# What GpSimd waits for while it scatters the input rows of a routed FFN

## The chip, the cores and the metric

One Trainium2 chip, one core. The metric is the device time of one execution in microseconds. The runs of the kernel before have a median of 1396.52 us (three runs, 1396.34 to 1397.36).

## The reference

Four sequences of 512 tokens with 256 values each (2048 rows, float32) pass through four residual layers, each behind a layernorm:

```python
x = x + attn_a(layernorm(x))        # 32 query heads, 8 key heads, rotary, causal
x = x + ffn(layernorm(x))           # routed
x = x + attn_b(layernorm(x))        # 16 differential heads, causal
x = x + ffn(layernorm(x))           # the same weights again
```

The FFN has 16 experts of inner width 176. Each token chooses four of them (out of its two best groups of four). With weights from a softmax over all experts,

```python
y = sum over the 4 chosen e of weight[e] * W2[e] @ (silu(W1[e] @ x) * (W3[e] @ x))
z = Ws2 @ (silu(Ws1 @ x) * (Ws3 @ x))      # the shared expert, inner width 352, every token
out = y + z
```

## The kernel before

The kernel is written engine by engine. Each engine has one list of instructions in program order, and the lists meet in semaphores: an instruction adds to one when it is done, and another engine's `wait_ge` holds that engine until the value is reached. Here are the parts of an FFN layer. The first FFN is called "f" in the code, the second "h".

**Seam.** TensorE projects the attention's output tile by tile, VectorE adds it to x, ScalarE normalises, and TensorE computes the router's logits. A row of `y_sb` then holds the normalised input (256 values), four slot numbers, four weights and the token's own row number: 265 values, 1060 bytes.

**Routing.** VectorE chooses the experts (`choose`), and `assign` (L1313) turns the choices into slot numbers in `slot_i`. Slots are places in the DRAM array `x_slots`, in which the rows of one expert lie together. `e_slots` goes up once for each half of the 16 tiles of 128 tokens.

**Dispatch.** GpSimd (`pool_ffn`) issues 64 indirect DMAs at L675, one for each tile of 128 tokens and each of the four choices. Each writes 128 rows of 1060 bytes from `y_sb` to the places given in `slot_i`. Scatter n belongs to tile n // 4. The first 40 (EARLY_T = 10 tiles) add to semaphore `scat0` when they land, the last 24 to `scat1`, 16 for each DMA. Between them stand waits: the table SHARED_AT names eleven scatters (8, 12, ..., 48), and before each of them GpSimd waits at L674 until the shared expert has come a given number of steps (`f_hw_used` or `h_hw_used`).

**Shared expert.** It runs at the same time in 12 steps, three for each sequence. In a step TensorE computes both inner products (L1909, eight matmuls), ScalarE applies the SiLU (L879), VectorE multiplies (L1414), and TensorE multiplies with Ws2 (L1919, eight matmuls, then `hw_used` goes up). After every third step VectorE adds the result to x (L1402). VectorE's remaining routing work (`full_tiles`, `places`, `order`) is spread between these steps.

**Experts.** The slots form 72 tiles of 128 rows, dealt with in 36 pairs. SyncE (`sp_ffn_slots`) waits for the landing of all 40 early scatters, then for each tile j reads the tile's first row from SBUF into a register (L490) and loads the tile into one of eight buffers `xg` (L465). With every second tile it also reads the expert's number (L511) and loads a part of that expert's W2 (L512). Before tile 4 it stores the last quarter of x (L486). Tiles from 24 on (EARLY) may also hold late tokens, so before tile 24 SyncE waits for `scat1`. Ahead of the steady work for the first pair, SyncE thus goes through: load 0, load 1, late weights, load 2, load 3, late weights, store of x, load 4, load 5. TensorE transposes each tile (L1941), multiplies with W1 and W3 (L1966), transposes the product (L1973), and multiplies with W2 (L1999 to L2004). Its loop for pair p begins with the transposes of pair p+2. ScalarE empties the transposes (L883) and applies the SiLU (L888), VectorE multiplies (L1439, L1442), finds each row's weight and destination (L1468 to L1482), and scales the result into one of eight buffers `yt` (L1456). Eight of the 72 tiles hold two experts' rows and have a second scatter.

**Results.** GpSimd adds each result tile to the output rows in DRAM, with 80 indirect accumulating DMAs at L691 (`scatter_out`). They stand behind the dispatch's 64 scatters in GpSimd's list. VectorE may fill a `yt` buffer again only when the scatter of its tile eight places before has landed. At the end SyncE loads the sums back (L524).

The change touches `pool_ffn` alone, and in it `scatter`:

```python
if n in SHARED_AT:
    pool.wait_ge(sm(f + "_hw_used"), 2 + SHARED_AT[n])
```

Of the kernel before, what the change touches and what calls it, by code (L numbers as in the profile page):

```python
# [26 lines left out]
NT = B * TB  # L27
# [26 lines left out]
TOPK = 4  # L54
# [19 lines left out]
EARLY_T = 10  # L74
# [5 lines left out]
assert EARLY * P <= EARLY_T * P * TOPK - NE * (P - 1)  # L80
SCH = [(0, 128), (128, 128), (256, 96)]
M_DMAS = 2 * 16
SHARED_AT = {8: 2, 12: 3, 16: 4, 20: 5, 24: 6, 28: 7, 32: 8, 36: 9, 40: 10, 44: 11, 48: 12}


class Chain:
# [13 lines left out]
def build(nc, ins, out):  # L100
    ctx = ExitStack()
    with ctx:
# [3 lines left out]
        def sem(name):  # L106
            return ctx.enter_context(nc.semaphore(name))
# [157 lines left out]
        def sm(name):  # L265
            if name not in S:
                S[name] = sem(name)
            return S[name]
# [65 lines left out]
        def past(f, n):  # L334

            return n if f == "h" else 0
# [331 lines left out]

        def pool_ffn(pool, f):

            def scatter(n):
                t, k = n // TOPK, n % TOPK
                if n in SHARED_AT:
                    pool.wait_ge(sm(f + "_hw_used"), 2 + SHARED_AT[n])  # L674
                pool.indirect_dma_start(x_slots, bass.IndirectOffsetOnAxis(ap=slot_i[:, t, k:k + 1], axis=0),  # L675
                                        y_sb[:, t, :], None).then_inc(sm("scat0" if t < EARLY_T else "scat1"), 16)

            outs = [(j, h) for j in range(NJ) for h in range(1 + (j in MIX))]

            def scatter_out(s):  # L680


                if s >= ACCS:
                    i, h = outs[s - ACCS]
                    if h == 0:
                        pool.wait_ge(sm(f"store{i % XR}"), 16 * (i // XR + 1 + past(f, NJ // XR)))
                    else:
                        pool.wait_ge(sm("store_second"), 16 * (MIX.index(i) + 1 + past(f, MIXED)))
                j, h = outs[s]
                to = j if h == 0 else NJ + MIX.index(j)  # L690
                pool.indirect_dma_start(y_acc[f][s % ACCS], bass.IndirectOffsetOnAxis(ap=dest[:, to:to + 1], axis=0),  # L691
                                        yt[:, j % XR, :], None, compute_op=ALU.add)\
                    .then_inc(sm(f"store{j % XR}" if h == 0 else "store_second"), 16)

            def result_out(j):
                pool.wait_ge(sm("e_dest"), j // 4 + 1 + past(f, NJ // 4))
                pool.wait_ge(sm("e_y_ev"), j + 1 + past(f, NJ))
                if j == 0:
                    pool.wait_ge(sm("acc_x"), 16 * B * (1 + past(f, 1)))
                scatter_out(outs.index((j, 0)))  # L700
                if j in MIX:
                    scatter_out(outs.index((j, 1)))

            pool.wait_ge(sm("e_slots"), 1 + past(f, 2))
            pool.wait_ge(sm("cleared"), 16 * (SLOT_ROWS // (4 * P) + 22))
            for n in range(TH * TOPK):
                scatter(n)
            pool.wait_ge(sm("e_slots"), 2 + past(f, 2))
            for n in range(TH * TOPK, NT * TOPK):
                scatter(n)  # L710
            for j in range(NJ):
                result_out(j)

        @block.gpsimd
        def _(pool):
            pool.memset(zero, 0.0).then_inc(sm("zeroed"), 1)

            pool.memset(v_all[:, :, :, D:D + 1], 1.0).then_inc(sm("a_ones"), 1)
            pool.wait_ge(sm("a_ones"), 1)
            pool_attn(pool, "a")  # L720
            pool_ffn(pool, "f")
            pool_back(pool)
            vo = v_all.rearrange("p g t (h c) -> p g t h c", h=2)
            pool.memset(vo[:, :, :, :, 16:17], 1.0).then_inc(sm("b_ones"), 1)
            pool.wait_ge(sm("b_ones"), 1)
            pool_attn(pool, "b")
            pool_ffn(pool, "h")
# [1388 lines left out]
```

## Time and profile before

| | us |
|---|---|
| median of three runs | 1396.52 |
| the profiled execution | 1398.89 |
| its span in the profile | 1397.2 |
| busy in the span: TensorE | 1153.5 (83%) |
| VectorE | 873.7 (63%) |
| GpSimd | 689.9 (49%) |
| ScalarE | 542.6 (39%) |
| DMA bytes, mean rate | 177.42 MB, 127 GB/s |

The profile shows one execution. PE is TensorE, DVE VectorE, ACT ScalarE, POOL GpSimd, SP SyncE; a "q" behind a name is the engine's instruction queue (waits, register work, DMA issues). Times are microseconds from the start of the span. In a timeline a row has start, duration (of the whole group, where several instructions are merged), engine, line, operation, output<-input, count, and in square brackets how long the engine was idle before and what ended that. "issue" means that the profile shows nothing it waited for, "remote" that the release came from no instruction the profile could name. The busy time of a GpSimd scatter is the time to make its descriptors, not that of the transfer. The two FFN layers begin their dispatch at 404.5 and 1087.0 us.

### The profile page before, as it was taken

The page shows a single profiled execution, that of the slowest core. Times are in us where ns is not written, and L with a number is a line of the kernel's source. Part 1 is how long each engine was busy: PE and PEld are TensorE (multiplying, and loading weights), DVE is VectorE, ACT ScalarE, POOL GpSimd, SP SyncE. Part 2 cuts the span into 40 slices and gives each one's busy share as a digit, 9 for nine tenths or more (in the row PEclk, how much of TensorE's full clock was granted, in tenths as well). Part 3 has the DMA queues.
Part 4 walks back from the last instruction along what each step waited for, and adds up shares of the span by engine and source line. Part 5 has one row for each costly group of instructions (what it writes and reads, how often), then busy time and mean ns, then how long its engine had stood idle before and what let it go on. Part 6 is the DMA issues. An engine that isn't in the chain of part 4 may idle for free.

```text
span 1397.2 us, 25837 instructions
## 1 busy us (share of the span) xinstructions
PE 1153.5 (83%) x8690; PEld 619.0 (44%) x8690; DVE 873.7 (63%) x2061; ACT 542.6 (39%) x846; POOL 689.9 (49%) x841
## 2 busy tenths in 40 slices
PE   6888899997888469999568799999878974999990
PEld 2343343332754246665233344444246542666550
DVE  5588888881783035555288799999567611555453
ACT  2125777778511012222122377777844100222210
POOL 4452344454036736677553355454520674667771
PEclk9887999999889679999779999999998995999995
DMA  4424655510813358888664422221062334788868
GB/s 148 130 83 146 191 185 180 160 44 26 287 42 121 133 125 151 151 153 145 110 194 152 149 54 54 61 58 51 3 233 47 109 128 129 140 152 154 156 91 255
DMA packets 154353, 177.42 MB, mean 127 GB/s; under 512 B 20016, under 2 KB 139760, under 8 KB 153712
## 3 DMA queue, kind: packets, MB, share of 16 engines
q1 hardware_dynamic: 124336, 136.38, 33.2%
q0 software_dynamic: 29184, 38.36, 16.2%
q8 instruction: 73, 1.20, 0.3%
q10 hardware_dynamic: 704, 1.02, 0.2%
q14 instruction: 56, 0.46, 0.1%
HBM read 91.12 MB, written 83.78 MB: 125 GB/s over the span
## 4 chain that ended last, share of the span: by engine, by line
PE 54%; DVE 17%; issue 8%; SPq 5%; ACT 5%; DMA 4%; POOL 4%; another core or an unknown queue 1%; POOLq 0%; ACTq 0%; DVEq 0%
PE pair_ps L1966 11%; PE o_ps L1737 8%; DVE nm L1106 4%; PE pair_ps L1999 4%; ACT arena L832 3%; DVE bm L1106 3%; POOL x_slots L675 3%; PE pair_ps L2002 2%; PE t_ps L1763 2%; PE pair_ps L1687 2%; PE pair_ps L1568 2%; PE pair_ps L1973 2%; DMA arena<-mT 2%; PE pair_ps L1662 2%; PE pair_ps L1667 2%
## 5 line engine op out<-in xcount | busy, mean ns | idle before, releaser
L832 ACT ACTIVATE arena<-pair_ps 128x1024 f32<-128x1024 f32 x320 | 323.5, 1025 | 134.0 <-PE pair_ps L1662 79.4
L615 POOL TENSOR_SCALAR_AFFINE_SELECT arena<-arena 128x512 f32<-128x512 f32 (+1 forms) x320 | 175.8, 549 | 243.2 <-ACT arena L832 242.7
L1106 DVE TENSOR_REDUCE nm<-pair_ps 128x2 f32<-128x1024 f32 (+1 forms) x192 | 232.9, 1222 | 37.2 <-PE pair_ps L1711 33.6
L675 POOL DMA_INDIRECT x_slots<-y_sb,slot_i x128 | 123.5, 965 | 168.7 <-DVE slot_i L1313 117.7
L1737 PE MATMUL o_ps<-arena 128*9 128x512 f32 (+7 forms) x2048 | 177.0, 441 | 4.3 <-POOL arena L615 4.1
L1966 PE MATMUL pair_ps<-arena 128*128 x512 | 170.1, 474 | 6.1 <-issue 6.1
L691 POOL DMA_INDIRECT y_f<-xnT,dest x80 | 125.0, 1563 | 72.4 <-DVE xnT L1456 51.7
L691 POOL DMA_INDIRECT y_h<-xnT,dest x80 | 124.7, 1559 | 67.9 <-DVE xnT L1456 43.5
L1106 DVE TENSOR_REDUCE bm<-pair_ps 128x8 f32<-128x1024 f32 x128 | 155.4, 1218 | 4.5 <-PE pair_ps L1711 1.0
L1439 DVE TENSOR_TENSOR arena<-arena,pair_ps 128x128 f32<-128x128 f32 x144 | 41.5, 288 | 128.5 <-ACT arena L888 77.3
L1966 PEld LDWEIGHTS pair_ps<-arena 128*128 128x128 f32 x512 | 95.2, 197 | 48.6 <-issue 11.8
L888 ACT ACTIVATE arena<-pair_ps 128x176 f32<-128x176 f32 x144 | 45.7, 318 | 168.4 <-PE pair_ps L1966 84.2
L1909 PE MATMUL pair_ps<-arena 128*128 128x512 f32 (+1 forms) x192 | 92.2, 627 | 0.0
L1456 DVE TENSOR_SCALAR xnT<-pair_ps,slot_w 128x256 f32<-128x256 f32 x144 | 64.5, 480 | 42.0 <-PE pair_ps L2004 24.0
L1711 PE MATMUL pair_ps<-c_b 64*128 64x128 bf16 (+1 forms) x1280 | 85.1, 210 | 0.0
L1711 PEld LDWEIGHTS pair_ps<-c_b 64*128 64x128 bf16 x1280 | 60.8, 98 | 33.8 <-issue 4.7
L1687 PE MATMUL pair_ps<-arena 48*128 48x512 bf16 x256 | 51.6, 397 | 20.8 <-ACT arena L832 16.5
L1662 PE MATMUL pair_ps<-arena 51*128 51x512 bf16 x256 | 51.2, 396 | 21.3 <-DMA arena<-mT 8.6
L879 ACT ACTIVATE sil<-pair_ps 128x512 f32<-128x512 f32 (+1 forms) x24 | 14.2, 596 | 124.7 <-PE pair_ps L1909 80.9
L1737 PEld LDWEIGHTS o_ps<-arena 128*9 128x9 f32 (+1 forms) x2048 | 39.0, 93 | 53.3 <-issue 30.3
L1999 PE MATMUL pair_ps<-arena 128*128 x224 | 59.1, 386 | 0.0
L883 ACT ACTIVATE arena<-t_ps 128x512 f32<-128x512 f32 x36 | 21.5, 597 | 96.8 <-PE t_ps L1941 78.1
(273 smaller groups left out, 2020.5 us busy)
## 6 DMA issues: line engine op xcount, KB each, us to landing
arena<-x_slots SPq DMA_DIRECT2D x128, 132.5 KB
arena<-in_w SPq DMA_DIRECT2D x4, 2816.0 KB, 19.2
x_slots<-hw SPq DMA_DIRECT2D x19, 530.0 KB, 3.7
arena<-q_a SPq DMA_DIRECT2D x64, 96.0 KB
arena<-q_b SPq DMA_DIRECT2D x64, 96.0 KB
y_f<-hw SPq DMA_DIRECT2D x11, 512.0 KB, 4.2
y_h<-hw SPq DMA_DIRECT2D x11, 512.0 KB, 4.2
arena<-in_w SPq DMA_DIRECT2D x2, 2048.0 KB, 17.4
```

Of the source, the lines that this page charges most:

```text
L615: pool.affine_select(p, p, pattern, ALU.is_ge, 0.0, base=0, channel_multiplier=-1)\
L675: pool.indirect_dma_start(x_slots, bass.IndirectOffsetOnAxis(ap=slot_i[:, t, k:k + 1], axis=0), y_sb[:, t, :], None).then_inc(sm("scat0" i ...
L691: pool.indirect_dma_start(y_acc[f][s % ACCS], bass.IndirectOffsetOnAxis(ap=dest[:, to:to + 1], axis=0), yt[:, j % XR, :], None, compute_op ...
L832: act.activation(p_ring[:, U % RING, :], pair_ps[:, pair_at("T", n, u)].rearrange("p a c -> p (a c)"), ACT.Exp, scale=SCALE).then_inc(sm(" ...
L1106: dve.tensor_reduce(dst, src, X, ALU.max, negate=not 2 <= u < 4).then_inc(sm("t_max_done"), 1)
L1662: mm = pe.matmul(ps, k_of(s, g, h, KM, 0, P), q_of(g, h, KM, 0, T), start=True, stop=True, skip_group_check=True)
L1687: pe.matmul(ps, q_of(g, h, KQ, 3 * P, T), k_of(s, g, h, KQ, 0, T), start=True, stop=False, skip_group_check=True)
L1711: mm = pe.matmul(blocks[:, :, 64 * half:64 * half + 64], mask_h[lo:lo + 64, half * P:half * P + P], ident_b[lo:lo + 64, lo:lo + 64].unsque ...
L1737: mm = pe.matmul(o_ps[32 * h:32 * h + vw, T - c:T], v_all[:, g, TB * b + j, v0:v0 + vw], p_ring[:, U % RING, a:a + c], start=j == 0, stop= ...
L1909: mm = pe.matmul(st_ps[0:m, k % 2, 512 * a:512 * a + 512], ws13[:, a, e, r:r + m], xnT_all[:, e, b * T:(b + 1) * T], start=e == 0, stop=e ...
L1966: mm = pe.matmul(s_ps[:, j % 2, 0:2 * INTER], xgT[:, j // 2 % 2, j % 2, c, :], w13[:, c, ds(e, 1), :].rearrange("p a i -> p (a i)"), start ...
L1999: pe.matmul(st_ps[:, h, 512:512 + E], hsT[:, h, :], w2[:, 0, ds(e, 1), :].rearrange("p a d -> p (a d)"), start=True, stop=False, skip_grou ...
```

## The change

The table SHARED_AT and the eleven waits on the shared expert go. In their place GpSimd waits before scatters 8, 16, 24, 32, 40, 48 and 56 until all preceding scatters of this layer have landed: the wait is for the full count of `scat0` (for scatters up to 40) or of `scat1` (for 48 and 56) up to scatter n-1. `past(f, k)` is k in the second FFN layer and 0 in the first, since the semaphores count on.

```diff
-SHARED_AT = {8: 2, 12: 3, 16: 4, 20: 5, 24: 6, 28: 7, 32: 8, 36: 9, 40: 10, 44: 11, 48: 12}
+BURST = 8

         def pool_ffn(pool, f):

+            def landed(n):
+                early = EARLY_T * TOPK
+                if n < early:
+                    pool.wait_ge(sm("scat0"), 16 * (n + 1 + past(f, early)))
+                else:
+                    pool.wait_ge(sm("scat1"), 16 * (n + 1 - early + past(f, NT * TOPK - early)))
+
             def scatter(n):
                 t, k = n // TOPK, n % TOPK
-                if n in SHARED_AT:
-                    pool.wait_ge(sm(f + "_hw_used"), 2 + SHARED_AT[n])
+                if n > 0 and n % BURST == 0:
+                    landed(n - 1)
                 pool.indirect_dma_start(x_slots, bass.IndirectOffsetOnAxis(ap=slot_i[:, t, k:k + 1], axis=0),
                                         y_sb[:, t, :], None).then_inc(sm("scat0" if t < EARLY_T else "scat1"), 16)
```

## Rows read from the trace of the kernel before

**Rows 1.** The page, part 4: shares of the chain that ended last, by engine.
```profile
PE 54%; DVE 17%; issue 8%; SPq 5%; ACT 5%; DMA 4%; POOL 4%; another core or an unknown queue 1%; POOLq 0%; ACTq 0%; DVEq 0%
```

**Rows 2.** Busy time by stretch: the expert phase of the first FFN.
```profile
core 0: us, PE busy (x) PEld busy (x) DVE busy (x) ACT busy (x) POOL busy (x), PEclk, DMA share, GB/s
...
510.00:687.00 177.00, 171.14 (x844) 105.96 (x842) 90.05 (x323) 42.00 (x101) 123.09 (x80) 0.99 0.80 137
```

**Rows 3.** Instructions of L675, both layers: duration, and idle time by releaser.
```profile
L675 POOL DMA_INDIRECT x_slots<-y_sb,slot_i x128: 957/963/1168, 404.5 to 1173.9; - x128
...
  remote: 14.6, 7
```

**Rows 4.** Timeline of GpSimd, first layer: scatters 0, 16, 32 and 63.
```profile
404.48 1.17 POOL L675 DMA_INDIRECT x_slots<-y_sb,slot_i  x1 [59.70 <-DVE slot_i L1313]
...
427.36 0.96 POOL L675 DMA_INDIRECT x_slots<-y_sb,slot_i  x1 [2.67 <-remote]
...
450.82 0.96 POOL L675 DMA_INDIRECT x_slots<-y_sb,slot_i  x1 [3.48 <-remote]
...
490.11 0.96 POOL L675 DMA_INDIRECT x_slots<-y_sb,slot_i  x1 [0.30 <-issue]
```

**Rows 5.** Timeline of GpSimd, second layer: scatters 0, 16, 32, 48 and 63.
```profile
1086.95 1.06 POOL L675 DMA_INDIRECT x_slots<-y_sb,slot_i  x1 [57.96 <-DVE slot_i L1313]
...
1109.84 0.96 POOL L675 DMA_INDIRECT x_slots<-y_sb,slot_i  x1 [2.81 <-remote]
...
1132.59 0.96 POOL L675 DMA_INDIRECT x_slots<-y_sb,slot_i  x1 [2.77 <-remote]
...
1154.90 0.96 POOL L675 DMA_INDIRECT x_slots<-y_sb,slot_i  x1 [2.25 <-remote]
...
1173.91 0.96 POOL L675 DMA_INDIRECT x_slots<-y_sb,slot_i  x1 [0.31 <-issue]
```

**Rows 6.** Timelines of TensorE, ScalarE and VectorE during the dispatches.
```profile
408.18 3.60 PE L1909 MATMUL pair_ps<-arena 128*128 128x512 f32 x8
...
418.61 3.60 PE L1909 MATMUL pair_ps<-arena 128*96 128x512 f32 x8
...
1145.80 1.03 PE L1919 MATMUL o_ps<-arena,hw 96*128 96x256 f32 x4
...
411.81 0.60 ACT L879 ACTIVATE sil<-pair_ps 128x512 f32<-128x512 f32 x1 [4.57 <-PE pair_ps L1909]
...
427.21 0.59 ACT L879 ACTIVATE sil<-pair_ps 96x512 f32<-96x512 f32 x1 [7.96 <-remote]
...
1154.66 0.75 DVE L1402 TENSOR_TENSOR x_sb<-x_sb,t_ps 128x256 f32<-128x256 f32 x2 [9.94 <-remote]
```

**Rows 7.** Chain that ended last, in order of time: around scatter 39's landing.
```profile
462.54 0.49 SPq L490
...
1141.55 3.24 DMA x_slots<-y_sb,slot_i
...
1144.80 0.46 SPq L490
```

**Rows 8.** Timeline of SyncE: three pairs of row-tile loads.
```profile
483.79 9.10 SPq L465 DMA_DIRECT2D arena<-x_slots  x2
...
497.32 1.91 SPq L465 DMA_DIRECT2D arena<-x_slots  x2
...
1157.46 3.58 SPq L465 DMA_DIRECT2D arena<-x_slots  x2
```

**Rows 9.** TensorE sees load 5 (timeline); its steady pace (chain).
```profile
501.10 0.69 PE L1941 MATMUL t_ps<-c_f,arena 128*128 128x128 f32 x2 [0.65 <-DMA arena<-x_slots]
...
1179.94 0.69 PE L1941 MATMUL t_ps<-c_f,arena 128*128 128x128 f32 x2 [4.90 <-DMA arena<-x_slots]
...
513.95 2.37 PE pair_ps L1966 x8
518.73 2.37 PE pair_ps L1966 x8
```

## The prediction, made before the change was run

> **What bounds the kernel now.** I read the chain of waits first, by engine: TensorE carries 54% of it, GpSimd 4% and issue time 8% [rows 1]. Then the table by stretches: the expert phase, 510 to 687 us, keeps TensorE busy for 171.14 of 177 us, GpSimd for 123.09 [rows 2]. Whatever moves that phase's start moves the end. GpSimd's 80 output scatters there need 123.09 + 80 x 0.30 = 147 us, so it has some 30 us to spare. Each dispatch must therefore be judged by when TensorE reaches the steady pace of the experts, 4.78 us a pair of tiles (513.95 to 518.73) [rows 9].
>
> Next the dispatch itself. One L675 scatter occupies GpSimd 0.963 us [rows 3]; from 450.82 to 490.11 there are 31 steps of 1.267 us with no stop [rows 4]. There are stops of another kind, put down to "remote": 14.6 us in 7 times over both layers [rows 3]. Five are large: 2.67 and 3.48 in the first layer, 2.81, 2.77 and 2.25 in the second [rows 4, 5]. They come at scatters 16 and 32 and, in the second layer, 48.
>
> Those stops are the clue. They wait for TensorE's shared-expert progress, which was long there. In the first layer scatter 16 wants the fourth step of the output matmuls; its matmuls had given way to those at 418.61 [rows 6], and scatter 16 started at 427.36. At the same moment others wake: the SiLU for the matmuls that ended at 418.61 + 3.60 = 422.2 started at 427.21, 5.0 us late, while the one for the matmuls that ended at 411.78 started at 411.81, at once [rows 6]. In the second layer VectorE saw TensorE's last shared step (1145.80 + 1.03 = 1146.8) at 1154.66, 7.8 us late, just when GpSimd's stop ended [rows 6]. So after about eight scatters in a row news between engines falls behind, and it catches up when GpSimd stops. Prompt at position 6 of the burst, 5.0 us late at position 15.
>
> SyncE suffers with them. It starts at the landing of scatter 39 (L490 at 462.54 and 1144.80) [rows 7] and has nine steps to do before steady work: six row-tile loads, two late-weight loads, one store of x. The second pair of loads needed 9.10 us [rows 8]; after the last scatter a pair takes 1.91 (497.32). TensorE sees load 5 only at 501.10 and 1179.94 [rows 9], 38.6 and 35.1 us after scatter 39 landed. **The dispatch bounds the start of the experts, but through slow SyncE and late semaphores more than through its own length.**
>
> **The change, part by part.**
>
> Removed: 11 waits a layer on the shared expert (scatters 8 to 48, every fourth). The two and three that stopped GpSimd give back, above the usual 0.30 us, 2.37 + 3.18 = 5.6 us in the first layer and 2.51 + 2.47 + 1.95 = 6.9 us in the second. The others cost nothing: the step goes on at 1.267 us.
>
> Added: seven waits a layer, at scatters 8, 16, ..., 56, for the preceding scatter's landing. Price from both sides: scatter 39 of the first layer starts at 450.82 + 7 x 1.267 = 459.69 and SyncE passes at 462.54, 2.85 us; in the second the chain gives 1141.55 to 1144.80, 3.25 us [rows 7]. Both are bursts of eight, as the new ones will be. With about 0.2 us to restart, a waiting step takes 3.05 to 3.45 us in place of 1.267: +1.8 to +2.2, I take 2.0, so 14 us a layer. A burst and its wait last 7 x 1.267 + 3.27 = 12.1 us. Queued behind the wait are only the later scatters and, behind scatter 63, the output scatters; those are covered by GpSimd's 30 us.
>
> What it does to three points. The last scatter starts at 490.11 + 14 - 5.6 = 498.5 and 1173.91 + 14 - 6.9 = 1181.0 [rows 4, 5]. Scatter 39 has landed at 404.48 + 39 x 1.267 + 4 x 2.0 + 3.05 = 464.9 (2.4 later) and 1086.95 + 60.5 = 1147.4 (2.6 later). News between engines is fresh at every burst's start, so the shared expert loses its stops; that gain is hidden, since load 0 still waits for scatter 39.
>
> The gain: SyncE's steps. Bounds for one: drained, two loads in 1.91 us with the issue of the steps between, about 1.2 us; in a burst, 1157.46 + 3.58 for two loads, that is 3.6 us from one to the next [rows 8]. The burst that showed 3.6 is the nearest kind, but it began right after a stop of 2.25 us without being emptied; each new burst begins with its queue empty and is over after eight. I take 2.2 us as the mean over burst and stop. Nine steps and the last load's 2 us are 21.8 us: TensorE sees load 5 at 486.7 and 1169.2. Until the dispatch has ended and drained (3 us after the last scatter's start, 501.5 and 1184.0) there are 14.8 us; at three steps a pair (6.6 us) TensorE does 2.24 pairs, worth 2.24 x 4.78 = 10.7 us of steady work. More than four pairs can't be done, since the eight output tiles are emptied only by scatters queued behind number 63.
>
> Sum: the first layer reaches that point at 501.5 instead of 501.10 + 10.7 = 511.8, a gain of 10.3; the second at 1184.0 instead of 1190.6, 6.6. Together -17 us, all on the path, because the steady phase behind it is TensorE's. Against the profiled execution (span 1397.2, its own time 1398.9) that is 1381.9; the median of the runs is 2.4 lower, so 1379.5.
>
> GpSimd's rows put a landing at 2.85 to 3.25 us after its issue. The Trainium skill (DMA: Bandwidth & Descriptors, Rules for kernel authors) says to issue a DMA early and wait on its semaphore late, so that the fixed cost overlaps: by that rule this change is a plain loss, which is the second rival below. The same page's anatomy of a GpSimd DMA gives about 2.0 us plus bytes by 436 GB/s, as an estimate 2.3 us for 136 KB. A wait would then add 1.2 us and not 2.0, and both dispatches together would end 11 us earlier; the trace shows 0.5 to 0.9 us more, and the sum goes by the trace.
>
> **The rivals.**
>
> *Bursts of eight never fall behind.* For it: the SiLU at position 6 was prompt. Then SyncE's steps take near 1.2 us, TensorE does its four pairs by the dispatch's end and stops at the output tiles: 501.10 + 19.1 - 501.5 = 18.7, and 1179.94 + 19.1 - 1184.0 = 15.0, together -34 us: 1363. Against it: the pair at 1157.46, slow from 2 us into a burst.
>
> *The dispatch's end sets the start (the slower side).* Place: SyncE's register loads and issues at L465 and L490. If they crawl whenever scatters are in flight, whatever the burst, the steady pace keeps its distance to the last scatter: 501.10 - 490.11 = 11.0 us after it in the first layer (some 5 of it the backlog of 32 scatters, so 6 now), 6.0 in the second. That gives 504.5 (+3.4) and 1187.0 (+7.1), together +10.5: 1407. This holds the forecast's rule out of play from about 3.6 us a step: nine steps then use up the bursts after scatter 39. For it: that same pair in the second layer; against it: the late news of rows 6, which grows with the length of the burst (nothing at position 6, 5.0 us at 15).
>
> *Gain and wait cancel.* With steps of 3 us, TensorE sees load 5 some 5 us earlier than before, and the ends lie near 1394 to 1399. This also takes in the case that the new wait's release is itself late (3.5 us or more a wait, as the old stop of 3.48) and the bursts stretch to 13 us.
>
> That the change doesn't do what it says I rule out: all seven thresholds are reached by scatters already issued, and each covers all of them.
>
> **How the numbers follow.** Forecast case (-9 to -27) 0.55; bursts always fresh 0.18; cancelled 0.11; dispatch's end 0.16. The range of 8 in 10 takes the forecast case, most of the fresh one and the cancelled one: 1362 to 1400. About 0.2% (2.8 us) is what a measurement of this kernel can tell from no change: faster by more 0.76, within it 0.07, slower 0.17.
>
> **What would show it.** GpSimd's idle before L675: seven gaps a layer of 2 to 2.5 us with a DMA as releaser, last scatter starting near 498 and 1181 counted from this profile's dispatch starts. SiLU rows at L879 right behind their matmuls. SyncE's L465 issues before the last scatter: about ten instead of three and four. L1966 running in groups of eight before the last scatter, and output scatters at L691 back to back (1.87 us) at first, with no idle 18 us ahead of them. Wrong would be: load 5 seen only after the last scatter; gaps over 3.5 us; or an expert phase that starts earlier and then waits for GpSimd at L691.

## The result and the profile after

The changed kernel took 1382.92 us in the median of four runs (1381.00 to 1384.67), beside 1396.94 us for the kernel before: ratio 0.9887, 95% interval 0.9849 to 0.9925. A later comparison gave 0.9883 (0.985 to 0.9916). The forecast was 1379.5 us. The profiled execution took 1384.51 us, its span 1382.8 us, against 1398.89 and 1397.2 before. This holds for the chips of those comparisons; the last experiments met another kind of chip, on which no run showed a gain from such waits.

| profiled execution, us | before | after |
|---|---|---|
| start of dispatch 1 to start of dispatch 2 | 682.5 | 672.3 |
| start of dispatch 2 to the end of the span | 310.3 | 306.1 |
| idle put down to "remote", sum over the 200 largest groups | 172.1 | 32.3 |

Scatters are now at L684, output scatters at L700, the first expert matmuls at L1975. The chain by engine answers to [rows 1]:

```profile
PE 50%; DVE 18%; issue 8%; POOL 6%; DMA 6%; SPq 6%; ACT 5%; another core or an unknown queue 0%; POOLq 0%; ACTq 0%; DVEq 0%
```

All instructions of L684, with what ended the idle time before them, answer to [rows 3]:

```profile
L684 POOL DMA_INDIRECT x_slots<-y_sb,slot_i x128: 957/963/1175, 404.5 to 1169.8; - x128
...
  issue: 34.3, 112
  DMA x_slots<-y_sb,slot_i: 30.9, 14
```

The releaser "remote" is gone from the scatters. Fourteen gaps that end with a landing took its place; above the usual 0.30 us they cost 30.9 - 4.2 = 26.7 us, 13.4 a layer. The timeline of GpSimd in the first dispatch has scatters 0, 8, 32 and 56, and answers to [rows 4]:

```profile
404.47 1.17 POOL L684 DMA_INDIRECT x_slots<-y_sb,slot_i  x1 [60.79 <-DVE slot_i L1322]
416.79 0.96 POOL L684 DMA_INDIRECT x_slots<-y_sb,slot_i  x1 [2.05 <-DMA x_slots<-y_sb,slot_i]
...
453.00 0.96 POOL L684 DMA_INDIRECT x_slots<-y_sb,slot_i  x1 [3.02 <-DMA x_slots<-y_sb,slot_i]
...
489.56 0.96 POOL L684 DMA_INDIRECT x_slots<-y_sb,slot_i  x1 [2.07 <-DMA x_slots<-y_sb,slot_i]
```

Scatter 63 follows at 498.43, 8.3 us later than before. ScalarE's SiLUs answer to [rows 6]: idle 4.56 to 4.77 us between them from 411.45 on, none late.

```profile
416.62 0.60 ACT L888 ACTIVATE sil<-pair_ps 128x512 f32<-128x512 f32 x1 [4.57 <-PE pair_ps L1918]
421.89 0.59 ACT L888 ACTIVATE sil<-pair_ps 96x512 f32<-96x512 f32 x1 [4.67 <-PE pair_ps L1918]
427.05 0.60 ACT L888 ACTIVATE sil<-pair_ps 128x512 f32<-128x512 f32 x1 [4.57 <-issue]
```

SyncE's row-tile loads answer to [rows 8]. Before, a pair took 9.10 us late in the dispatch; now the first four pairs of layer 1 take 1.4 to 1.5 us each (in layer 2 the second, third and fourth pair take 2.59, 1.59 and 2.21):

```profile
465.35 1.51 SPq L465 DMA_DIRECT2D arena<-x_slots  x2
...
468.74 1.43 SPq L465 DMA_DIRECT2D arena<-x_slots  x2
...
475.76 1.43 SPq L465 DMA_DIRECT2D arena<-x_slots  x2
...
479.06 1.43 SPq L465 DMA_DIRECT2D arena<-x_slots  x2
```

TensorE sees load 5 at 479.16 (501.10 before [rows 9]). What becomes of those 22 us can be read from its groups of eight matmuls with W1 and W3, one group for each pair of tiles, counted from 1. These are, in FFN layer 1, groups 2 to 8 of the changed kernel, then of the kernel before (its groups 4 to 6 stand 4.78 us apart between the rows shown):

```profile
481.20 4.00 PE L1975 MATMUL pair_ps<-arena 128*128 x8
...
487.44 2.53 PE L1975 MATMUL pair_ps<-arena 128*128 x8
...
496.33 4.90 PE L1975 MATMUL pair_ps<-arena 128*128 x8
...
504.21 2.56 PE L1975 MATMUL pair_ps<-arena 128*128 x8
...
511.48 2.53 PE L1975 MATMUL pair_ps<-arena 128*128 x8
...
516.26 2.53 PE L1975 MATMUL pair_ps<-arena 128*128 x8
...
522.65 2.53 PE L1975 MATMUL pair_ps<-arena 128*128 x8
```

```profile
503.07 3.68 PE L1966 MATMUL pair_ps<-arena 128*128 x8
...
509.00 2.53 PE L1966 MATMUL pair_ps<-arena 128*128 x8
...
528.12 2.53 PE L1966 MATMUL pair_ps<-arena 128*128 x8
...
532.90 2.53 PE L1966 MATMUL pair_ps<-arena 128*128 x8
```

Group 2 comes 21.9 us earlier, group 3 21.6, group 7 11.9, group 8 10.2, and there it stays. In layer 2, counted from the dispatch's start, group 2 gains 17.5 us and group 7 4.0. About half or more of the head start is given back around the end of the dispatch, where ScalarE again shows late news:

```profile
503.19 0.32 ACT L897 ACTIVATE arena<-pair_ps 128x176 f32<-128x176 f32 x1 [3.95 <-remote]
506.95 0.60 ACT L892 ACTIVATE arena<-o_ps 128x512 f32<-128x512 f32 x1 [3.45 <-remote]
```

Scatters 56 to 63 are followed at once by output scatters (L700 at 499.69, 501.61, ...), so the last burst is longer than eight. That is not the whole of it: part of the head start is lost earlier, inside the bursts of eight, as the account of the prediction shows below.

### The profile page after: what moved, and what is told of

Read it like the earlier page. It is cut to its first block, busy times and chain, and to the rows that moved or that the text cites. A ratio compares the mean times of both kernels' runs of the same rounds, so it can differ in the third digit from the quotient of the medians.

```text
span 1382.8 us, 25837 instructions
## 1 busy us (share of the span) xinstructions
PE 1160.6 (84%) x8690; PEld 623.0 (45%) x8690; DVE 873.2 (63%) x2061; ACT 542.9 (39%) x846; POOL 690.0 (50%) x841
## 4 chain that ended last, share of the span: by engine, by line
PE 50%; DVE 18%; issue 8%; POOL 6%; DMA 6%; SPq 6%; ACT 5%; another core or an unknown queue 0%; POOLq 0%; ACTq 0%; DVEq 0%
PE pair_ps L1975 9%; PE o_ps L1746 8%; POOL x_slots L684 5%; DVE nm L1115 4%; ACT arena L841 4%; PE pair_ps L2008 3%; DVE bm L1115 3%; PE pair_ps L2011 2%; PE t_ps L1772 2%; DMA x_slots<-y_sb,slot_i 2%; PE pair_ps L1696 2%; PE pair_ps L1577 2%; DMA arena<-mT 2%; PE pair_ps L1982 2%; PE pair_ps L1671 2%
## 5 line engine op out<-in xcount | busy, mean ns | idle before, releaser
L684 POOL DMA_INDIRECT x_slots<-y_sb,slot_i x128 | 123.7, 967 | 185.2 <-DVE slot_i L1322 120.0
L1975 PE MATMUL pair_ps<-arena 128*128 x512 | 174.1, 483 | 2.2 <-issue 2.2
L700 POOL DMA_INDIRECT y_h<-xnT,dest x80 | 124.7, 1559 | 57.8 <-DVE xnT L1465 34.8
L700 POOL DMA_INDIRECT y_f<-xnT,dest x80 | 125.0, 1563 | 53.8 <-DVE xnT L1465 31.1
L1975 PEld LDWEIGHTS pair_ps<-arena 128*128 128x128 f32 x512 | 97.3, 202 | 46.3 <-issue 10.7
L2008 PE MATMUL pair_ps<-arena 128*128 x224 | 60.6, 393 | 5.4 <-issue 3.6
## 6 DMA issues: line engine op xcount, KB each, us to landing
arena<-in_w SPq DMA_DIRECT2D x2, 2048.0 KB, 17.5
```

The costliest lines, as they stand in the source:

```text
L1975: mm = pe.matmul(s_ps[:, j % 2, 0:2 * INTER], xgT[:, j // 2 % 2, j % 2, c, :], w13[:, c, ds(e, 1), :].rearrange("p a i -> p (a i)"), start ...
L2008: pe.matmul(st_ps[:, h, 512:512 + E], hsT[:, h, :], w2[:, 0, ds(e, 1), :].rearrange("p a d -> p (a d)"), start=True, stop=False, skip_grou ...
```

## The experiments

Each kernel ran beside the kernel before on the same chip. Edits are against the changed kernel; where one uses SHARED_AT, the table stands in the file again, which the lines shown here leave out. All ratios are to the kernel before.

| run | edit | us | before there | ratio, 95% interval |
|---|---|---|---|---|
| no_waits | no stops | 1460.29 | 1392.35 | 1.0489 (1.0463 to 1.0514) |
| burst16 | landing wait every 16 | 1425.74 | 1392.35 | 1.024 (1.0212 to 1.0267) |
| burst4 | landing wait every 4 | 1389.42 | 1392.35 | 0.9981 (0.9965 to 0.9996) |
| drain_last | one more, after scatter 63 | 1373.3 | 1392.35 | 0.9867 (0.9847 to 0.9887) |
| changed_again | none | 1381.63 | 1398.77 | 0.9883 (0.985 to 0.9916) |
| stop_without_landing | stop, no landing | 1379.35 | 1398.77 | 0.988 (0.9841 to 0.9918) |
| landing_waits_late | new waits from 40 on | 1375.74 | 1398.77 | 0.9855 (0.9817 to 0.9894) |
| tiny_scatters | no stops, 4 bytes a row | 1462.5 | 1398.77 | 1.0456 by one execution |
| spread_stops | short memset before each scatter | 1350.89 | 1340.53 | 1.0087 (1.0056 to 1.0117) |
| landing_waits_early | new waits up to 32 | 1355.23 | 1340.53 | 1.0117 (1.0086 to 1.0148) |
| late8_and_drain | late ones, and after 63 | 1342.4 | 1340.53 | 1.0019 (1.0001 to 1.0036) |
| spread_then_landing | memsets in layer 1, landing waits in layer 2 | 1356.93 | 1342.83 | 1.0097 (1.0076 to 1.0118) |

### Are stops needed, and how often?

This is the edit of no_waits; burst16 has 16 in that place, burst4 has 4.

```diff
-BURST = 8
+BURST = 64
```

> The changed kernel with no waits between scatters at all (neither the shared expert's progress nor landings). Theory (bursts of more than about eight scatters let semaphores and SyncE fall behind, and a stop lets them catch up): the dispatch ends 7 x 1.8 = 12 us earlier in each layer (last scatter near 484), but SiLUs at L888 come late from scatter 10 on, by 5 us and more, the shared expert ends after 465 in place of 456, SyncE's steps crawl at 3 to 4 us, and TensorE sees load 5 only after the last scatter has drained, near 495 to 500. Time 1390 to 1410, slower than the changed kernel. Rival (the gain came from taking away the waits on the shared expert, which had stopped GpSimd for 5.6 and 6.9 us): these stops are gone here too and the landing waits with them, so the time falls below the changed kernel's, to 1355 to 1372.

> The changed kernel with BURST = 16: waits for landings at scatters 16, 32 and 48 alone. That is nearly the pattern of stops which the kernel before had by chance (16 and 32, in the second layer 48 too). Theory: SiLUs late by 2 to 6 us at the ends of the bursts, SyncE's nine steps take some 25 to 33 us, time 1388 to 1397, near the kernel before. Rival (the removed waits on the shared expert were the cost): about 1375, below the changed kernel, since four landing waits of 1.8 us fewer a layer are made.

> The changed kernel with BURST = 4: 15 waits a layer in place of 7. The dispatch ends some 8 x 1.8 = 14 us later in each layer (last scatter near 513). Theory: news stays fresh, SyncE's steps take 1.2 to 1.4 us, TensorE reaches its four pairs and then waits for the output tiles until the dispatch is over, so part of the longer dispatch is seen: 1390 to 1402. If the gain grew only with the number of stops, it would be below 1383.

ScalarE's SiLUs without any stop:

```profile
417.13 0.60 ACT L888 ACTIVATE sil<-pair_ps 128x512 f32<-128x512 f32 x1 [5.12 <-PE pair_ps L1918]
452.17 0.59 ACT L888 ACTIVATE sil<-pair_ps 96x512 f32<-96x512 f32 x1 [34.44 <-remote]
492.07 0.60 ACT L888 ACTIVATE sil<-pair_ps 128x512 f32<-128x512 f32 x1 [39.31 <-remote]
```

The scatters themselves run freely, the last at 484.20, 14 us before the changed kernel's. But the shared expert, whose matmuls and SiLUs wait for each other, advances two steps in 75 us. SyncE's first row-tile load goes out at 514.64, the first output scatter at 538.79. The direction was expected, the size was not: +4.9%. So the waits that the change removed were not idle: something must stop GpSimd.

What is late is not only news from another engine. VectorE's routing steps L1384 to L1387 wait for nothing but VectorE's own preceding step, through a semaphore; here they start at 419.26, 419.94, 420.64 and 421.34, 0.70 us apart, where in the kernel before the same steps (L1375 to L1378) stood 0.20 to 0.31 us apart. Whether the semaphores are updated late or the waiting queues go slowly, no run separates.

In burst16 each of the three landing waits stops it for only 1.81, 2.25 and 1.74 us, and the SiLUs fall ever further behind:

```profile
425.00 0.59 ACT L888 ACTIVATE sil<-pair_ps 96x512 f32<-96x512 f32 x1 [12.52 <-remote]
...
468.72 0.59 ACT L888 ACTIVATE sil<-pair_ps 96x512 f32<-96x512 f32 x1 [17.01 <-remote]
491.13 1.08 ACT L888 ACTIVATE sil<-pair_ps 128x512 f32<-128x512 f32 x2 [21.82 <-remote]
```

That expectation was wrong: I had put burst16 level with the kernel before, which also runs sixteen scatters at a stretch. The difference is what the stop waits for. A landing wait ends 1.7 to 2.3 us after its scatter, whatever ScalarE has heard by then. The old wait ended when TensorE's own late news had come through (2.67 and 3.48 us [rows 4]); it lasted as long as needed. This reading agrees with both traces; no run separates it further.

burst4 came out 0.6 us below the expected 1390 to 1402, with the last scatter at 512.21 (513 expected). Its SiLUs are prompt, but GpSimd sits idle 64.6 us at its thirty waits, 55.6 more than the usual 0.30 us each, so the gain of fresh news is nearly used up.

### Is it the landing, the bytes, or the stop?

```diff
-                    landed(n - 1)
+                    for i in range(3):
+                        pool.memset(idle[:], 0.0).then_inc(sm("idle"), 1)
+                        pool.wait_ge(sm("idle"), 3 * (n // BURST - 1) + i + 1 + past(f, 21))
```

> The changed kernel with each of its seven waits for a landing replaced by three small memsets on GpSimd, one after the other, some 1.8 us in all: GpSimd stops issuing for as long as before, but waits for nothing. Theory (what helps is the stop, in which the other engines' semaphores get through): as the changed kernel, ratio to the kernel before 0.985 to 0.995, SiLUs prompt. Rival (what helps is that scatters have landed, so that few are in flight): like the kernel without waits, ratio 1.02 to 1.05.

```profile
412.23 1.70 POOL L685 MEMSET idle<- 128x512 f32 x3
414.21 0.97 POOL L687 DMA_INDIRECT x_slots<-y_sb,slot_i  x1 [0.28 <-POOL idle L685]
```

Three memsets, 1.70 us of GpSimd's own work, do what the landing wait does: ScalarE sits idle 4.25 to 4.99 us between SiLUs, and 0.988 beside the changed kernel's 0.9883 on the same chip. **It is the stop that helps, not the knowledge that rows have landed.**

```diff
-BURST = 8
+BURST = 64
...
-                pool.indirect_dma_start(x_slots, bass.IndirectOffsetOnAxis(ap=slot_i[:, t, k:k + 1], axis=0),
-                                        y_sb[:, t, :], None).then_inc(sm("scat0" if t < EARLY_T else "scat1"), 16)
+                pool.indirect_dma_start(x_tiny, bass.IndirectOffsetOnAxis(ap=slot_i[:, t, k:k + 1], axis=0),
+                                        y_sb[:, t, 0:1], None).then_inc(sm("scat0" if t < EARLY_T else "scat1"), 16)
```

> No waits between scatters (as in the run without waits), and each scatter moves 4 bytes a row in place of 1060, into another DRAM array; so the experts see zeros and every result goes to the rows that are thrown away. The number of rows, descriptors and semaphore increments stays. If the bytes hold up the other engines' news, SiLUs are prompt, the dispatch ends at 484, the shared expert at 456, and the time is below 1380. If descriptors and increments do it, SiLUs start 30 us late and more again, as at 452 and 492 in the run without waits, and the time is above 1440.

This kernel writes only one element of each row, to a tensor of its own, and the experts read rows that nobody filled; its total tells nothing of their work. Its SiLUs stand at 416.91, 451.99 and 491.92, within 0.3 us of those of no_waits. So what delays the news does not depend on the bytes of a scatter. It is something that each scatter or each of its 128 rows brings along; which of the two was not tried.

### Where in the dispatch does the gain arise?

```diff
+                if n in SHARED_AT and n < 40:
+                    pool.wait_ge(sm(f + "_hw_used"), 2 + SHARED_AT[n])
-                if n > 0 and n % BURST == 0:
+                if n >= 40 and n % BURST == 0:
                     landed(n - 1)
```

> The kernel before (waits on the shared expert at scatters 8 to 36), with landing waits at scatters 40, 48 and 56 in place of its waits at 40, 44 and 48. Theory: the gain lies behind scatter 39, where SyncE's nine steps run; here the dispatch has the old stops at 16 and 32 and the new ones at 40, 48 and 56, ends 3 to 5 us earlier than the changed kernel's, and SyncE's steps are as quick: ratio to the kernel before 0.984 to 0.991. Rival (the seven waits must stand all along, since the shared expert's delays count): 0.995 to 1.003.

```profile
422.44 0.96 POOL L687 DMA_INDIRECT x_slots<-y_sb,slot_i  x1 [2.75 <-remote]
446.06 0.96 POOL L687 DMA_INDIRECT x_slots<-y_sb,slot_i  x1 [3.65 <-remote]
457.67 0.96 POOL L687 DMA_INDIRECT x_slots<-y_sb,slot_i  x1 [1.78 <-DMA x_slots<-y_sb,slot_i]
```

With the old stops and the old late SiLUs (443.85 after 12.85 us) up to scatter 39, and landing waits at 40, 48 and 56 alone, the ratio is 0.9855. So the whole gain lies behind scatter 39; the mirror of this run, with the new waits up to 32 alone, met another kind of chip (below) and can't confirm it. The dispatch lasts 91.9 us, 2.0 less than the changed kernel's, where 3 to 5 were expected. The earlier end of the shared expert (456.5 against 463.5) is worth nothing, as predicted.

```diff
             for n in range(TH * TOPK, NT * TOPK):
                 scatter(n)
+            landed(NT * TOPK - 1)
```

> The changed kernel with one more wait in each layer: GpSimd waits for the landing of scatter 63 before the first output scatter. In the changed kernel eight input scatters are followed at once by four or more output scatters (L700), and the step from the third to the fourth group of L1975 takes 11.6 us in the second layer and 7.9 in the first in place of 4.8, with SiLUs and transposes seen 2 to 4 us late. Theory: that is the same falling behind, in a burst of eight made longer; a stop of 1.8 us there removes some of it, 3 us a layer at most less than the changed kernel: 1377 to 1383. Rival (these delays are only due to the output tiles or to SyncE's loads): no gain, or 1 to 4 us slower.

> The changed kernel itself, unaltered, beside the others on this chip: a ratio to the kernel before of 0.987 to 0.992, as at first. It is the measure for the ratio of 0.9867 that the wait behind scatter 63 had: if that wait gained nothing, both ratios agree within 0.002; if it gained what its trace shows, this one is higher by 0.003 to 0.006.

In the profiled execution the first output scatter waits 3.57 us (502.76), and from the dispatch's start TensorE reaches group 8 of layer 1 after 516.88 - 405.52 = 111.4 us against 522.65 - 404.47 = 118.2, and group 7 of layer 2 after 109.3 against 116.2. So these two executions differ by 6.8 us a layer where the long last burst was suspected. But changed_again is there after 116.5 and 113.9 us: two executions of one and the same kernel differ by 1.7 and 2.4 us. The idle time put down to "remote" is 8.3 us with the wait and 25.0 in changed_again. The timed ratios, 0.9867 and 0.9883 on two chips, differ by 0.2% with overlapping intervals. I call the gain of this wait undecided.

### Another kind of chip

The last four kernels met two chips on which the kernel before takes 1340.53 and 1342.83 us, not 1392 to 1399. Neither was met a second time, so that the difference belongs to the chip, and not to its state at the time, is not shown; "kind of chip" below stands for either.

```diff
-BURST = 8
+W = 64
...
-                if n > 0 and n % BURST == 0:
-                    landed(n - 1)
+                if n > 0:
+                    pool.memset(idle[:, :W], 0.0).then_inc(sm("idle"), 1)
+                    pool.wait_ge(sm("idle"), n + past(f, 63))
```

> The landing waits are taken away and one short memset of 128x64 (an estimate of 0.2 us, from the 334 ns of a 128x128 one) with a wait for its end stands ahead of each scatter but the first, so the period is about 1.49 us instead of 1.267 and the stops sum to about the 14 us a layer that the seven landing waits take. Theory A (the scatters' news is worked off at a rate a little slower than one per 1.267 us, and only the mean rate counts): prompt SiLUs, last scatter near 498 us, time 1375 to 1388, like the changed kernel. Theory B (other engines' news goes through only in an unbroken stop of a microsecond or more, and a steady stream holds it up at any rate): the SiLUs come 20 us or more late as without waits, 1420 to 1460. Rival C: 0.2 us a scatter is too little but helps in part: 1395 to 1420.

Then landing_waits_early:

```diff
+                if n in SHARED_AT and n >= 40:
+                    pool.wait_ge(sm(f + "_hw_used"), 2 + SHARED_AT[n])
-                if n > 0 and n % BURST == 0:
+                if 0 < n < 40 and n % BURST == 0:
                     landed(n - 1)
```

> The mirror of the run with the late landing waits: landing waits at scatters 8, 16, 24 and 32, the old waits on the shared expert at 40, 44 and 48. Theory (what the change gains is gained behind scatter 39, where the kernel before runs eight to sixteen scatters with SyncE and TensorE late): about as the kernel before, ratio 0.993 to 1.002, TensorE's first look at load 5 at 482 to 488 us. Rival (the earlier end of the shared expert is what brings the gain): ratio 0.985 to 0.990.

And late8_and_drain:

```diff
+                if n in SHARED_AT and n < 40:
+                    pool.wait_ge(sm(f + "_hw_used"), 2 + SHARED_AT[n])
-                if n > 0 and n % BURST == 0:
+                if n >= 40 and n % BURST == 0:
                     landed(n - 1)
...
                 scatter(n)
+            landed(NT * TOPK - 1)
```

> The old waits on the shared expert below scatter 40, landing waits at 40, 48 and 56, and a wait for the landing of the last scatter before the first output scatter. If the last burst and the output scatters that follow it hold up the first layer-one matmuls of the experts (the third to fourth group takes 11.6 us in layer 2 against 4.8 us later), the wait gives back 2 to 8 us: 1368 to 1375, ratio 0.980 to 0.985. If what these pairs wait for is the rate of the loads alone: 1374 to 1380, as the run without that wait (ratio 0.9855).

Every expectation of the three missed, since each was made for chips with late news. None of the four profiles has any "remote" idle in its 200 largest groups. late8_and_drain still has the old waits at 8 to 36, and they stop nothing there. Of its 128 scatters:

```profile
  DVE slot_i L1326: 115.9, 2
  issue: 36.3, 119
  DMA x_slots<-y_sb,slot_i: 14.3, 6
  PE o_ps L1932: 0.3, 1
```

Its SiLUs run past scatter 16 without delay, where [rows 6] had one 5.0 us late:

```profile
415.60 0.60 ACT L892 ACTIVATE sil<-pair_ps 128x512 f32<-128x512 f32 x1 [4.57 <-PE pair_ps L1922]
420.87 0.59 ACT L892 ACTIVATE sil<-pair_ps 96x512 f32<-96x512 f32 x1 [4.67 <-PE pair_ps L1922]
426.03 0.60 ACT L892 ACTIVATE sil<-pair_ps 128x512 f32<-128x512 f32 x1 [4.57 <-PE pair_ps L1922]
```

The scatters take their 963 ns on both kinds. What is missing here is the lateness, and with it the gain of such waits. The early waits are then plain loss: eight gaps of 17.3 us, less 8 x 0.30, are 14.9 us, and the run is 1.17% of 1340.5 = 15.7 us slower. They stand ahead of scatter 39, and load 0 waits for that scatter. The late waits and the wait after scatter 63 cost next to nothing, 1.0019.

The dispatch's neighbourhood also holds nearly the whole difference between the chips. late8_and_drain takes as long as the kernel before on its chip (1.0019), so its trace can stand for that one. From dispatch 1 to dispatch 2 it takes 651.8 us, landing_waits_late 669.4, the kernel before on its own chip 682.5; from dispatch 2 to the end 283.7 against 310.3 before. Of those two differences, 30.7 and 26.6 us, 29.0 and 26.3 have arisen when TensorE reaches group 8 (after 99.4 and 98.7 us against 128.4 and 125.0).

spread_stops answered nothing of its question, since without lateness both theories expect prompt SiLUs. So the last kernel holds two dispatches: the short memsets in layer 1, the seven landing waits in layer 2.

```diff
-                if n > 0 and n % BURST == 0:
+W = 64
...
+                if n > 0 and past(f, 1) == 0:
+                    pool.memset(idle[:, :W], 0.0).then_inc(sm("idle"), 1)
+                    pool.wait_ge(sm("idle"), n)
+                if n > 0 and n % BURST == 0 and past(f, 1) == 1:
                     landed(n - 1)
```

> Two dispatches in one kernel: in layer 1 the short memset of 128x64 ahead of every scatter and no landing wait, in layer 2 the seven landing waits of the changed kernel. It is read by layer. The three runs before it were taken on another chip, where the kernel before takes 1340.5 us and no news came late. Where the kernel before takes about 1395 us: Theory A (only the mean rate of scatters counts) expects prompt SiLUs at 5.2 us in layer 1, ratio 0.985 to 0.995; Theory B (engines' news needs an unbroken stop) expects SiLUs 20 us or more late in layer 1 and a ratio of 1.005 to 1.025, half of the loss without waits less layer 2's gain. Where the kernel before takes about 1340 us: both theories expect prompt SiLUs in both layers, layer 2 with seven waits of 1.8 to 3.3 us (14 to 17 us in sum) that bring the first-layer groups of the experts no earlier than in the runs with fewer landing waits, and a ratio of 1.007 to 1.015.

It met a chip of the same kind (1342.83 us). Layer 2 has the changed kernel's dispatch:

```profile
1099.66 0.96 POOL L689 DMA_INDIRECT x_slots<-y_sb,slot_i  x1 [1.73 <-DMA x_slots<-y_sb,slot_i]
1113.02 0.96 POOL L689 DMA_INDIRECT x_slots<-y_sb,slot_i  x1 [3.55 <-DMA x_slots<-y_sb,slot_i]
...
1124.72 0.96 POOL L689 DMA_INDIRECT x_slots<-y_sb,slot_i  x1 [1.79 <-DMA x_slots<-y_sb,slot_i]
1137.24 0.95 POOL L689 DMA_INDIRECT x_slots<-y_sb,slot_i  x1 [2.71 <-DMA x_slots<-y_sb,slot_i]
1149.49 0.95 POOL L689 DMA_INDIRECT x_slots<-y_sb,slot_i  x1 [2.46 <-DMA x_slots<-y_sb,slot_i]
```

From dispatch 2 to the end it takes 1354.6 - 1064.78 = 289.8 us, landing_waits_early 1351.4 - 1061.58 = 289.8, late8_and_drain 283.7. So the three later waits add nothing to the four early ones, which cost 6.1 us against the old waits in that place. The expected 1.007 to 1.015 held, at 1.0097. If layer 1 of the changed kernel goes the same way, the changed kernel takes on such a chip what landing_waits_early takes, about 1355 us, 1.2% more than before. The changed kernel itself was not run on such a chip, so that figure is an estimate.

Where the lateness exists, whether a steady stream at 1.41 us a scatter cures it as well as a stop every eight stays open: no run met such a chip.

## Why the prediction was right, and where it was not

**The stops.** Seven waits of 1.8 to 2.2 us above the usual gap were expected, 14 us a layer; they measured 13.7 and 13.0. The last scatter was put at 498.5 and started at 498.43; in layer 2, from the dispatch's start, 94.05 was expected and 93.04 measured. Scatter 39's landing was put at 464.9, and SyncE passed it at 464.35.

**Fresh news in bursts of eight.** The mechanism held for ScalarE (prompt SiLUs) and for SyncE up to load 5; remote idle fell from 172.1 to 32.3 us. But a burst of eight does not stay fresh for SyncE: its queue steps, which else take less than 0.5 us, come 0.70 us apart from the third to fifth scatter of the burst until the next stop. Five bursts behind scatter 39 show it (from 470.2 and 481.2 in layer 1, from 1142.9, 1152.7 and 1163.9 in layer 2). That stops decide what is late, no_waits, burst16 and stop_without_landing show from three sides. What I had not seen is the other half: the removed waits held the lateness in bounds, and the change works because it brings stops of its own.

**SyncE's step.** "I take 2.2 us as the mean over burst and stop" was too much. By the same count, nine steps and 2 us from 464.35 to 479.16, it is 1.42 us, near the drained end of 1.2. By itself this would have meant a larger gain. Behind load 5 it turned: from the issue of load 5 to that of load 9, two pairs on, SyncE took 14.7 us in layer 1 (476.86 to 491.58) and 17.3 in layer 2 (1150.10 to 1167.35), where the sum gives it 13.2.

**Pairs until the dispatch has drained.** Here the sum was too kind. Load 5 came 7.5 us before the forecast in layer 1 (6.8 in layer 2, from the dispatch's start), and yet layer 1 gained 10.2 us (10.3 forecast) and layer 2 4.2 (6.6 forecast). The step that failed is "at three steps a pair (6.6 us)" up to 3 us after the last scatter, with steady work behind it. In layer 2, groups 3, 4 and 5 start 11.2 and 11.6 us apart, reaching past the end of the dispatch:

```profile
1160.16 2.53 PE L1975 MATMUL pair_ps<-arena 128*128 x8
...
1171.36 3.66 PE L1975 MATMUL pair_ps<-arena 128*128 x8
...
1182.98 2.98 PE L1975 MATMUL pair_ps<-arena 128*128 x8
```

The first of the two intervals is over before the first output scatter has had any effect (it starts at 1171.06). Ahead of group 4 TensorE has the transposes of loads 8 and 9, and it waits for load 9, which SyncE issued late:

```profile
1167.35 0.01 SPq L465 DMA_DIRECT2D arena<-x_slots  x1
```

```profile
1169.22 0.69 PE L1950 MATMUL t_ps<-c_f,arena 128*128 128x128 f32 x2 [4.07 <-DMA arena<-x_slots]
```

SyncE had lost the time in the bursts of scatters 48 to 55 and 56 to 63, at 0.70 us a queue step. Between loads 8 and 9 its list also has four transfers of weights for a tile that holds two experts' rows (L476 to L481), which "three steps a pair" leaves out. On a chip without lateness, late8_and_drain needs 10.2 us from load 5 to load 9, these four included. In the second interval the last burst runs on into the output scatters, a burst longer than eight, which I had counted only as covered work; ScalarE empties transposes that ended at 1169.9 only at 1176.80, 6.9 us late. Layer 1 shows the same wait for load 9 (TensorE at 494.19, group 4 at 496.33). Two errors of opposite sign brought the sum within 3.4 us; that it was this near was in part luck.

**The sum.** Forecast -17 us from the profiled execution; its span lost 14.4, 10.2 + 4.2.

**The rivals.** Always fresh bursts (-34) failed: up to load 5 SyncE was nearly as quick as this rival wants (1.42 against 1.2 us a step), but inside the later bursts it was not, and the end of the dispatch held up the rest. The slower rival, in which the steady pace keeps its distance to the last scatter, did not come: load 5 is seen 19.3 us before the last scatter of layer 1. Yet the slower side exists, through another door: on a chip whose news is prompt, the early waits delay scatter 39, and load 0 with it. I had counted that delay (2.4 us) and called the traded gain larger, which holds only where the trace of before shows late news.

The Trainium skill (DMA: Bandwidth & Descriptors, Rules for kernel authors) says to issue early and wait late. On the second kind of chip the runs agree: four early waits cost 1.2%, late ones next to nothing. On the first kind they do not: with no wait at all the kernel is 4.9% slower, and what helps in a wait there is the stop itself.

## What to carry to other kernels

When other engines' rows turn "remote" and late behind a long run of GpSimd scatters, try a stop of about 1.7 us every eight and look at those rows, before removing any wait that seems redundant. Put such stops behind the last scatter that holds up other work; here those behind scatter 39 won as much as all seven (0.9855 against 0.9883), and those ahead of it cost 1% on chips without the lateness. Repeat the comparison on more than one chip: the same program differed by 4% between them, and with it what there was to gain.

## What the runs showed of the hardware that was not expected

- Behind scatters issued every 1.267 us without a stop, ScalarE sat idle for 34.4 and 39.3 us before two SiLUs, while the scatters kept their pace. The matmuls of the first had ended 30 us before (418.22 + 3.60 = 421.8 in no_waits, the SiLU at 452.17). It does not depend on the scatters' bytes (4 bytes a row do the same).
- A stop of 1.7 us every eight scatters keeps the SiLUs prompt, one of 1.7 to 2.3 us every sixteen does not.
- Even with stops every eight, SyncE's queue steps come 0.70 us apart in the later part of a burst, and so do VectorE's steps that wait for its own semaphore in no_waits. The chain of the changed kernel, in order of time, with one load's work strung out inside the burst that began at 477.66:

```profile
481.92 0.69 SPq L490
482.62 0.71 issue
483.37 0.71 SPq L465
```

- All this was seen where the kernel before takes 1392 to 1399 us, and none of it where it takes 1340 to 1343 us, with scatters of the same 963 ns. What distinguishes the chips, or whether one chip can be in both states, is not known from these runs.
